# VectorE takes the first tile's rows one step earlier, and more unread products on TensorE in three places

## The reference

```
x = x + 0.5 * ffn(layernorm(x));  x = x + attn(layernorm(x));  x = x + 0.5 * ffn(layernorm(x))

def ffn(x):      # 2 sequences of 256 in the source; here 1 of 1024 tokens
    h = x + attention(rmsnorm(x, n1))        # 16 heads, 4 key/value heads of 128, rotary, causal
    xt = rmsnorm(h, n2)
    topv, topi = top_k(xt @ gate_w, 2)       # 8 experts, 2 for each token, softmax of the two
    for e in range(8):                       # w1, w3: 256 x 512;  w2: 512 x 256
        out += w[:, e] * ((silu(xt @ w1[e]) * (xt @ w3[e])) @ w2[e])
    return h + out

def attn(x):     # token mixing
    x1 = ln(x); xln = ln(x1); mix = xln * tf + shift(xln) * (1 - tf)
    r = sigmoid(mix @ Wr)
    vmix = sum over t of (xln @ Wv)[t] * exp(decay * (T - 1 - t))
    x2 = x + r * (vmix @ Wo + bo)
    xc = ln(ln(x2)); kc = relu(shift(xc) @ Wck) ** 2
    return x2 + sigmoid(xc @ Wcr) * (kc @ Wcv)
```

## Time and profile before

| what | us |
|---|---|
| median of 3 runs | 1244.08 |
| lowest and highest of them | 1241.51 and 1373.93 |
| the profiled execution, its own time | 1240.9 |
| its span, first to last instruction | 1239.0 |
| TensorE busy | 1161.0 (94%) |
| VectorE busy | 938.8 (76%) |
| ScalarE busy | 798.4 (64%) |
| GpSimd busy | 569.1 (46%) |
| granted TensorE clock, mean over the span | 0.983 |

### The profile page before, as it was taken

The page is one execution under the profiler, slowest core; times in us unless marked ns, Lnnn a source line. Parts: engine busy times, 40 slices in busy tenths (PEclk is TensorE's granted clock), DMA queues, the critical chain, the costliest instruction groups (busy, mean ns, idle before and its releaser), DMA issues.

```text
span 1239.0 us, 18836 instructions
## 1 busy us (share of the span) xinstructions
PE 1161.0 (94%) x6558; PEld 975.0 (79%) x6558; DVE 938.8 (76%) x1992; ACT 798.4 (64%) x1573; POOL 569.1 (46%) x421
## 2 busy tenths in 40 slices
PE   4899999999999889996998899999999999899994
PEld 3788888888888568883687688888888888758883
DVE  6877887887897767768787777787787788677773
ACT  5766676676666467775565766666676666467773
POOL 3666666666640044430001495675675660025451
PEclk9999999999999999999999999999999999989997
DMA  4100100100013452242101000100100010761113
GB/s 138 39 1 1 39 1 1 39 1 1 2 52 132 158 174 65 65 137 89 56 1 48 26 1 1 26 14 1 27 13 2 1 52 1 248 197 53 52 52 123
DMA packets 48685, 65.93 MB, mean 53 GB/s; under 512 B 5840, under 2 KB 34384, under 8 KB 48464
## 3 DMA queue, kind: packets, MB, share of 16 engines
q1 hardware_dynamic: 42064, 50.56, 12.8%
q0 software_dynamic: 4416, 12.06, 3.2%
q10 hardware_dynamic: 2112, 2.10, 0.5%
HBM read 54.48 MB, written 10.22 MB: 52 GB/s over the span
## 4 chain that ended last, share of the span: by engine, by line
PE 45%; DVE 4%; ACT 2%; issue 1%; POOL 1%; DMA 1%; SPq 0%; DVEq 0%; ACTq 0%; POOLq 0%
PE ps L1639 11%; PE ps L1641 11%; PE ps L1640 11%; PE ps L1709 5%; PE ps L1793 3%; PE ps L1781 1%; PE ps L1620 1%; PE ps L1855 1%; DVE h L1221 0%; DMA mixT<-y_dram 0%; PE ps L1761 0%; ACT probs L813 0%; PE ps L1832 0%; DVE ps L1199 0%; POOL probs L685 0%
## 5 line engine op out<-in xcount | busy, mean ns | idle before, releaser
L813 ACT ACTIVATE probs<-ps,negmax 128x128 f32<-128x128 f32 (+7 forms) x256 | 189.7, 741 | 89.1 <-DVE negmax L1199 86.0
L819 ACT ACTIVATE probsT<-ps 128x512 fp32r<-128x512 f32 x288 | 170.3, 597 | 112.1 <-PE ps L1709 110.7
L1205 DVE TENSOR_TENSOR probsT<-ps,probsT 128x512 fp32r<-128x512 f32 x288 | 195.9, 685 | 46.4 <-ACT probsT L819 45.0
L1199 DVE CUSTOM_DVE_ANT_0 ps<-ps,causal 128x128 f32<-128x128 f32 (+7 forms) x256 | 193.4, 761 | 28.3 <-PE ps L1641 26.2
L689 POOL TENSOR_TENSOR crossed<-crossed,rope 128x512 f32<-128x512 f32 x70 | 90.3, 1290 | 191.4 <-ACT crossed L799 191.3
L1709 PE MATMUL ps<-square,probs 128*128 128x128 f32 x1152 | 170.9, 273 | 5.7 <-ACT probs L813 5.3
L1709 PEld LDWEIGHTS ps<-square,probs 128*128 128x128 f32 x1152 | 141.3, 141 | 35.1 <-issue 4.2
L736 POOL DMA_INDIRECT xs<-rows_dram,token_of x46 | 70.3, 1528 | 175.0 <-DVE token_of L1289 156.0
L1221 DVE SCALAR_TENSOR_TENSOR h<-ps,rowinv,h 128x256 f32<-128x256 f32 x256 | 123.3, 482 | 35.9 <-PE ps L1641 27.3
L1310 DVE TENSOR_TENSOR parts<-experts,parts 128x1024 fp32r<-128x1024 f32 x92 | 112.3, 1225 | 48.8 <-ACT parts L863 46.6
L1639 PE MATMUL ps<-keysT,queriesT 128*128 128x512 f32 (+4 forms) x384 | 141.9, 370 | 3.3 <-DVE straight L1175 1.4
(11 more groups left out here) (255 smaller groups left out, 2838.2 us busy)
## 6 DMA issues: line engine op xcount, KB each, us to landing
experts<-in_L_ffn_w_dram SPq DMA_DIRECT2D x48, 512.0 KB, 6.5
w_in<-in_L_ffn_wq_dram SPq DMA_DIRECT2D x8, 512.0 KB, 3.9
wo_in<-in_L_ffn_wo_dram SPq DMA_DIRECT2D x8, 512.0 KB, 6.1
rows_dram<-probs ACTq DMA_DIRECT2D x4, 512.0 KB, 3.0
probs<-y_dram SPq DMA_DIRECT2D x8, 256.0 KB, 4.3
mixT<-y_dram SPq DMA_DIRECT2D x8, 256.0 KB, 5.0
probs<-in_L_attn_x_dram SPq DMA_DIRECT2D x2, 512.0 KB, 4.5
w_in<-in_L_ffn_wk_dram SPq DMA_DIRECT2D x8, 128.0 KB, 5.0
```

What stands on the lines that cost most here:

```text
L813: act.activation(probs[:, i % 2, k, 0:w], ps[:, 2 * slot_n:2 * slot_n + 2, :].rearrange("p b n -> p (b n)")[:, at:at + w], ACT.Exp, bias=n ...
L819: act.activation(probsT[:, m % 3, 0, :], ps[:, 4 + m % 2, :], ACT.Copy).then_inc(S["probsT_high"], 1)
L1199: dve.tensor_tensor_reduce(out=row, in0=row, in1=causal[:, T - w:T], scale=-1.0, scalar=LARGEST, op0=ALU.add, op1=ALU.min, accum_out=negma ...
L1205: dve.tensor_tensor(probsT[:, m % 3, 1, :], ps[:, 4 + m % 2, :], probsT[:, m % 3, 0, :].bitcast(F32), ALU.subtract).then_inc(S["probsT_low ...
```

## The change

The low part of tile 0's rows comes ahead of both blocks of tile 1's weights on VectorE, in each moe(f); 20 unread products stand behind the inversion in place of 15, and 5 more, in bank 7, between tile 0's turned rows and its first product; and 70 stand ahead of the token mixing's first turn in place of 54.

```
-SPINS = (9, 18, 15, 54, 40, 12)
+SPINS = (9, 18, 20, 70, 40, 12)

                 dve.wait_ge(S["owner_ready"], f + 1)
                 e = expert(f, 1)
-                split_up(f, 1, 0, e)
                 take_xs(f, 0)
-                split_up(f, 1, 1, e)
+                for k in range(2):
+                    split_up(f, 1, k, e)
                 take_xs(f, 1)

                 spin(SPINS[2])
                 pe.wait_ge(S["owner_ready"], f + 1)
                 turn_xs(f, 0)
+                spin(5, 7)
                 up(f, 0)
                 up(f, 1)
```

## The result

| | us | ratio to before |
|---|---|---|
| before, median of 9 runs | 1242.71 | |
| changed, median of 9 runs (1235.19 to 1242.15) | 1238.15 | 0.9966 (0.9952 to 0.998) |
| changed, once more on another chip, 12 runs | 1240.21 | 0.9979 (0.9964 to 0.9993) |
| changed, the profiled execution | 1238.38 | |

The change makes the kernel 0.2% to 0.3% faster, 2.6 to 4.2 us; 2.65 had been worked out, and 1240 forecast. (The two medians of the table differ by 4.56; the ratio leaves out the run of 1373.93 as a slow one.) The span of the profiled execution went from 1239.0 to 1236.6.

What follows compares the result with a forecast made beforehand. TensorE, 45% of the span in the chain of waits, was taken as the bound. Terms -0.98 - 1.57 - 0.70 + 0.60 = -2.65 gave 1238.25 from the profiled time, 1241.4 from the median; forecast 1240 us, 8-in-10 range 1236 to 1246.

Steps and rivals of the forecast that it cites:

- (4): moe(1): clock falls under the 20 unread products, so turn and first product come later, +0.60 us; bounds +1.7 and -0.77.
- (1): moe(0): VectorE takes tile 0's rows right behind ScalarE, so the first product comes earlier, -0.98 us; moved blocks cost nothing.
- (2): moe(0): 20 and 5 unread products fit in idle time and keep the clock up in tile 0's products, -1.57 us.
- (3): Token mixing: 70 unread products keep the clock full; decayed sums start 0.26 earlier and run 0.44 shorter, -0.70 us.
- No delay: Token mixing: the sixteen additional unread products end at 586.77, ahead of the first turn at 587.03 by 0.26.
- the prediction's own sign: moe(0) or mixing: prediction wrong if unread products end behind what they cover, or tile 0's products show a 0.50 row.
- second rival: All three places: unread products at half clock become the queue; +1.75 us in all, 1242.7; chance 0.12.
- first rival: moe(1): clock does not fall under the unread products, -0.77 there, -4.02 in all, 1236.9 us; chance 0.2.
- slower rival: The second rival: half-clock unread products delay moe(0) +0.32, moe(1) +0.60, mixing +0.83; chance 0.12.
- The third: moe(0): unread products do not hold the clock, leaving (1), (3), (4): -1.08 us, 1239.8; chance 0.18.

Runs made afterwards that it cites:

- order_and_mixing: Changed kernel with 15 unread products behind the inversion and none behind the turn; new VectorE order and 70 kept: 1238.65 us, 0.9968 of before.
- order_only: Kernel before with VectorE's new order alone, still 15 and 54 unread products and none behind the turn: 1239.05 us, 0.9967 of before.
- no_five: Changed kernel without the five unread products between tile 0's turn and its first product: 1238.49 us, 0.9958 of before.
- fifteen: Changed kernel with 15 unread products behind the inversion in place of 20: 1237.35 us, 0.9962 of before.
- mixing_only: Kernel before with 70 unread products ahead of the token mixing's turns in place of 54: 1240.66 us, 0.9976 of before.
- overrun: Changed kernel with 40 unread products behind the inversion in place of 20: 1246.77 us, 1.0036 of before.
- third_buffer: `fifteen` with tile 2's rows gathered into a buffer of their own: 1236.13 us, 0.9962 of before.
- four_later: Changed kernel with the load of expert 4 and of x held back until tile 2's rows are turned: 1240.43 us, 0.9982 of before.

## Why the prediction was right, step by step

The range and the direction held, and the sum of -2.65 lies between the two comparisons. The steps did less well than the sum. That the sum came so near is in part luck: the errors of (4), +0.60 for a measured -0.19, and of what it did not look at (the stretch behind vmix, the opening of the program, the end of moe(1)) cancel in the profile. And 1240 rests on the 3.2 by which the median of three runs stood above the profiled one; with nine runs that median is 1242.71, 1.8 above it.

(1) VectorE's order: forecast -0.98 in moe(0), measured 5.74 against 6.67, -0.93; `order_and_mixing` has it to the hundredth (436.95 and 437.44). The blocks of tile 1, costed at nothing, cost nothing.

(2) "What they should return is the clock", -1.57: the size is right (7.26 against 8.77, -1.51), but the 20 and the 5 are not needed for it: `order_and_mixing` has 7.25 without them. In six stages with the old order and 15 unread products the products of tile 0 ran in part at half clock in four (8.71 to 8.77); with the new order and 15, in none of four (`order_only`, `order_and_mixing`); with the old order and 20 and 5, in none of two. All profiles with the new order and unread products behind the inversion together have none in 18 stages. That the order alone spares the fall is thus well borne out; that the 20 and the 5 alone do rests on two stages. Where the order has already spared it, they have nothing left to give, which fits `no_five` and `fifteen`.

This accounts for part of why 4.1, 2.5 and 3.0 us, each by itself, give only 2.6 to 4.2 together. It does not account for the 70, which act elsewhere: `order_only` gives 4.1 and `mixing_only` 3.0, but `order_and_mixing` only 4.0. The intervals (2.5 to 5.8, 1.1 to 4.9 and 2.2 to 5.7) are too wide to tell whether the 70 add anything on top of the order; in the times, the order alone is as good as the whole change.

(3) Token mixing: forecast -0.70, and just that in the profile (14.50 to 13.80). But it was worked out from the one execution shown, and over four profiles the fall costs 1.14 there. The 3.0 us of `mixing_only` hold also the stretch in attention(1), which the prediction did not see. "No delay" of the first turn was wrong. By the prediction's own sign it had one thing wrong here: the unread products end behind what they cover. In all ten profiles with 70 TensorE has no idle time ahead of the turns, and the first turn comes 1.06 to 1.74 behind the first normalised tile, against 0.65 to 0.66 in the four with 54. The margin of 0.26 was read from one execution, in which the sixteen products ahead of the 54 (L1900) took 5.21; in the changed kernel's profile they took 6.05, more of them at half clock (0.60 in the mean from 565.8 to 571.6, against 0.70 from 566.5 to 571.5 before). These rows also answer the second rival's "since they come behind steady work": the 54 ran at full clock although an idle time of 5.70 and a stretch at half clock lay shortly ahead of them. The delay is hidden behind ScalarE's four tiles in nine profiles (13.8) and costs 0.2 in the tenth (14.0).

(4) moe(1), +0.60: this is the term that failed. It supposed that the clock falls under the unread products as it did in the profile before. It fell under 20 of them in 2 of 10 stages, and under 15 in 4 of 14. Where it did, first product and turn came as worked out (7.00 for 6.99); where it did not, as in the changed kernel's profile, the first product came 0.93 earlier, and the first rival was the right one. Its -0.77 for that term then met the late gather of tile 2: 13.40 against 13.59, -0.19, in the profile. The -4.02 of that rival is near the 4.2 of the first comparison.

The slower rival had its mechanism (`overrun` shows its price), but not the three falls at once that it needed. The third did not come about either.

The profile's own difference, -2.4, is not the sum of these steps: -2.44 in moe(0), -0.70 in the mixing, -0.19 in moe(1) make -3.3. Attention(1) gained 1.49 and attention(0) lost 1.72, and 0.7 was lost behind moe(1)'s first down product, in tiles and transfers that no edit touches.

## What to carry to other kernels

When two edits are meant to cure the same stall, price them together: VectorE's order alone removed the fall of the clock here, and the additional unread products then had nothing left to remove. Put first the instruction that TensorE waits for; an order on VectorE that costs nothing did what unread work does at a risk. Unread products belong where the pause would otherwise be long, and in a number that ends before what they cover: 15 gained 3.0 us over none, 20 gained nothing over 15 that could be seen, and 40 cost 4 us in each stage. Take the margin for that number from several executions: the 0.26 of the 70 was gone in all ten profiles.

## What the runs showed of the hardware

The spread of this kernel's times comes in good part from falls of TensorE's clock that differ from one execution to the next. token_of of moe(0), ahead of which no kernel here was changed, came at 429.7 to 430.0 in the four profiles without a stretch at 1.2 GHz in attention(0) or the routing, and at 433.4 to 433.7 in the four with three (near 24, 44 and 423): 3.7 us, as much as the change gives. The single runs agree: those of `third_buffer` under 1237 us have a mean granted clock of 0.986 to 0.990, those over 1239 one of 0.979 to 0.984. In all fourteen profiles the idle time of 5.7 ahead of the products of L1900 brought a fall, which began between 560 and 567. With 54, the idle times of 2.4 to 3.7 ahead of the mixing's first turn had one at their end or about 2 us behind it in all four. That of 1.7 to 2.2 between tile 0's turn and its first product (old order, 15) had one in the products behind it in four stages of six, and that of 1.2 (new order, no five: `order_only`, `order_and_mixing`, `no_five`) in none of six.

A gather of 128 rows that took 2.8 to 3.0 us from issue to landing while nothing else was loaded took 5.6 to 7.6 as tile 2's, issued about 1 us behind the first of the expert loads. `four_later`, with three loads beside it, still had the late landing; whether the number of loads or only their being ahead counts was not tried further.
